# A macaron attention block on one core: the second query group's probabilities are turned by VectorE and transfers instead of TensorE

## The reference

```python
x = x + 0.5 * ffn(layernorm(x))        # 384 hidden, silu(gate) * up
x = x + attention(layernorm(x))        # 16 heads of 64, rotary, causal softmax
x = x + 0.5 * ffn(layernorm(x))
# attention, for each batch and head:
scores = where(causal, q @ k.T * 64 ** -0.5, -inf)
out = softmax(scores) @ v              # then the 16 heads side by side, @ wo.T
```

## Time and profile before

| | |
|---|---|
| median of 3 runs | 1251.76 us (1251.71 to 1252.58) |
| the profiled execution | 1256.88 us |
| its span | 1255.0 us |
| TensorE busy | 1220.6 us (97%), 7,264 matmuls |
| VectorE busy | 734.1 us (58%) |
| ScalarE busy | 892.1 us (71%) |
| GpSimd busy | 401.6 us (32%) |
| transfers | 164.84 MB, mean 131 GB/s |

### The profile page before, as it was taken

The page is one execution under the profiler, slowest core; times in us unless marked ns, Lnnn a source line. Parts: engine busy times, 40 slices in busy tenths (PEclk is TensorE's granted clock), DMA queues, the critical chain, the costliest instruction groups (busy, mean ns, idle before and its releaser), DMA issues. The chain is left out here.

```text
span 1255.0 us, 26509 instructions
## 1 busy us (share of the span) xinstructions
PE 1220.6 (97%) x7264; PEld 845.1 (67%) x7264; DVE 734.1 (58%) x1790; ACT 892.1 (71%) x1945; POOL 401.6 (32%) x223
## 2 busy tenths in 40 slices
PE   7996999999999999999999999999999999999898
PEld 4554776767676767676767777676767676766465
DVE  5565656565656565656566666556555656564454
ACT  4764777777777777777777777677777777777574
POOL 3343423332323333333333332323332333330000
PEclk8997999999999999999999999999999999999999
DMA  6236556565554555555555555546555455543000
GB/s 253 85 120 161 135 127 164 129 170 128 153 143 128 138 144 142 133 142 141 138 139 140 153 128 141 156 119 170 128 157 140 131 138 146 135 101 78 11 35 33
DMA packets 118606, 164.84 MB, mean 131 GB/s; under 512 B 14384, under 2 KB 64432, under 8 KB 118448
## 3 DMA queue, kind: packets, MB, share of 16 engines
q1 hardware_dynamic: 118176, 163.70, 49.2%
q10 hardware_dynamic: 400, 0.79, 0.3%
HBM read 53.02 MB, written 10.75 MB: 51 GB/s over the span
## 5 line engine op out<-in xcount | busy, mean ns | idle before, releaser
L1017 DVE CUSTOM_DVE_ANT_0 probs<-wide,tri_mask 128x1024 f32<-128x1024 f32 (+7 forms) x512 | 382.4, 754 | 251.0 <-PE wide L733 247.5
L922 ACT ACTIVATE shared_a<-bank 128x512 f32<-128x512 f32 (+2 forms) x640 | 338.5, 550 | 165.5 <-PE bank L749 159.6
L911 ACT ACTIVATE probs<-probs,neg_max 128x1024 f32<-128x1024 f32 (+7 forms) x512 | 394.5, 772 | 84.3 <-DVE neg_max L1017 82.1
L749 PEld LDWEIGHTS bank<-ident,probs 128*128 128x128 f32 x2304 | 259.5, 140 | 132.2 <-issue 70.1
L153 POOL TENSOR_TENSOR rotated<-terms,cross 128x1024 f32<-128x1024 f32 x62 | 148.5, 2396 | 613.0 <-DVE cross L147 612.8
L749 PE MATMUL bank<-ident,probs 128*128 128x128 f32 x2304 | 343.5, 278 | 1.1 <-ACT shared_a L922 0.4
L766 PE MATMUL bank<-shared_a,v_cur 128*64 128x256 f32 (+3 forms) x1792 | 297.3, 453 | 0.0
L732 PE MATMUL wide<-k_hh,q_hl 128*128 128x512 f32 (+3 forms) x768 | 288.8, 378 | 7.7 <-DMA k_low<-parts 5.5
L733 PE MATMUL wide<-k_low,q_hl 128*128 128x512 f32 (+3 forms) x768 | 255.7, 345 | 0.0
L766 PEld LDWEIGHTS bank<-shared_a,v_cur 128*64 128x64 f32 x1792 | 108.8, 136 | 121.8 <-issue 85.2
L732 PEld LDWEIGHTS wide<-k_hh,q_hl 128*128 128x128 f32 x768 | 146.3, 191 | 36.3 <-issue 24.1
(11 more groups left out here) (143 smaller groups left out, 1235.6 us busy)
## 6 DMA issues: line engine op xcount, KB each, us to landing
q_hl<-parts SPq DMA_DIRECT2D x254, 128.0 KB, 2.7
k_hh<-parts SPq DMA_DIRECT2D x254, 128.0 KB, 2.7
v_cur<-shared_b SPq DMA_DIRECT2D x32, 512.0 KB, 4.3
inv_sum<-inv_scratch SPq DMA_DIRECT2D x128, 128.0 KB, 3.1
k_low<-parts SPq DMA_DIRECT2D x63, 256.0 KB, 4.2
xn_cur<-xn_scratch SPq DMA_DIRECT2D x15, 1024.0 KB, 6.6
w_qk<-w_scratch SPq DMA_DIRECT2D x32, 256.0 KB, 3.1
w_scratch<-first_w_parts SPq DMA_DIRECT2D x8, 512.0 KB, 3.1
```

The costliest lines, as they stand in the source:

```text
L749: last = nc.tensor.transpose(ring[at % 2][:, col:col + P], probs[g][:, h, OFFSET[g][r] + j * P:OFFSET[g][r] + (j + 1) * P], ident[:])
L911: nc.scalar.activation(own, own, ACT.Exp, bias=neg_max[g][:, col], scale=-1.0, accum_out=sums[g][:, col]).then_inc(probs_done, 1)
L922: nc.scalar.activation(turned[:, slot, to], ring[at % 2][:, 0:w * len(heads)], ACT.Copy).then_inc(ring_free[at % 2], signals)
L1017: nc.vector.tensor_tensor_reduce(out=part_of_probs(g, k), in0=wide_banks[k % 2][:, x0:x1], in1=tri_mask[:, SEQ - (x1 - x0):], scale=1.0, s ...
```

## The change

Group 0 stays as it is, with its ten turns and a ring of 14 places a pair instead of 24. Group 1 has no turns by TensorE and no copies by ScalarE any more:

- `score` writes each unit of group 1 as two halves of equal width, one in each bank of the wide tile. Its keys come in another order: key 128 j + 64 b + 2 i + c goes to bank b, part c, block j, column i. The matmul's moving operand so reads every second float.
- The mask has that order too; VectorE and GpSimd set it up once. Probabilities go to `second`, four parts (b, c) of 32 columns for each block.
- `turn_blocks` on VectorE turns each square of 32 x 32 in place, one instruction for a unit, eight a pair.
- `send_second` on SyncE moves the squares: eight transfers for each of two sets (blocks 4 and 5 of both heads, then blocks 2 and 3), each from 32 partitions to 64, of 2,816 or 1,792 bytes for a partition, into `spread`, 16 transfers a pair.
- `times_v_second` multiplies in three steps, reading `spread` in runs of 32 columns and writing `out_bank` in the order quarter, block, row of the quarter. `normalise` puts the columns back.
- The q and k fills are issued for the whole sequence, 8 transfers a pair instead of 16. The inverses are spread as they lie in DRAM, without reordering.
- The hand-written orders of all four engines are changed to suit.

The core of the diff:

```diff
+def fill_qk_whole(queue, o, u, h):
+    for part in range(2):
+        to = slice(HEAD_DIM * part, HEAD_DIM * (part + 1))
+        queue.dma_start(o.q_hl[u][h][to, :].bitcast(F32), rows_of(o, h, part, slice(0, SEQ))).then_inc(o.filled_qk[u][0], 16)
+        queue.dma_start(o.k_hh[u][h][to, :].bitcast(F32), rows_of(o, 2 + h, 0, slice(0, SEQ))).then_inc(o.filled_qk[u][1], 16)
...
+        SECOND_STEPS = [(0, (0, 1, 2)), (0, (3, 4, 5)), (1, (0, 1, 2, 3))]
...
-                q = q_hl[u][h][:, P * TILES[g][r]:P * (TILES[g][r] + 1)]
-                x0, x1 = scores_at(g, k)
-                for a, b in ((x0, min(x1, CHUNK)), (CHUNK, x1)):
...
+                    else:
+                        high, low = (a[u][h][:, 0:P * n].rearrange("d (j b i c) -> d b c j i", b=2, i=HALF, c=2)[:, b] for a in (k_hh, k_low))
+                        out = wide_banks[k % 2][:, CHUNK * b:CHUNK * b + HEAD_DIM * n].rearrange("p (c j i) -> p c j i", c=2, i=HALF)
+                    nc.tensor.matmul(out, q, high, start=True, stop=False)
+                    last = nc.tensor.matmul(out, q, low, start=False, stop=True)
...
+            def times_v_second(p, u, d):
+                s, blocks = SECOND_STEPS[d]
+                if d == 0:
+                    may_multiply(p, 1)
+                pe.wait_ge(spread_full[s], 16 * SENDS * (p + 1))
+                for j in blocks:
+                    rows = [r for r in SET_ROWS[s] if TILES[1][r] >= j]
+                    for h in range(2):
+                        out = out_bank[HEAD_DIM * h:HEAD_DIM * (h + 1), :].rearrange("p (a r i) -> p a r i", a=QUARTERS, r=4)
+                        out = out[:, :, rows[0], :] if len(rows) == 1 else out[:, :, rows[0]:rows[-1] + 1, :]
+                        last = nc.tensor.matmul(out, v_cur[:, u, j, HEAD_DIM * h:HEAD_DIM * (h + 1)], spread_of(s, h, j, rows),
+                                                start=(j == 0), stop=(j == TILES[1][SET_ROWS[s][1]]))
+                last.then_inc(out_step, 1)
...
+            def turn_blocks(p, k):
+                dve.wait_ge(probs_done, unit(p, 1, k))
+                own = part_of_second(k)
+                nc.vector.transpose(own, own).then_inc(blocks_turned, 1)
...
+            def send_second(p, s):
+                sp.wait_ge(blocks_turned, 8 * p + 4 * (s + 1))
+                if some(p):
+                    settle(sp)
+                    sp.wait_ge(out_step, NK * (p - 1) + (NK - 1, NK)[s])
+                for a in range(QUARTERS):
+                    for b in range(2):
+                        sp.dma_start(spread[s][HEAD_DIM * b:HEAD_DIM * (b + 1), a, :],
+                                     second[s][HALF * a:HALF * (a + 1), 2 * b:2 * b + 2, :]).then_inc(spread_full[s], 16)
```

More of the change, by code:

```diff
@@ L905, in exponential @@
             def exponential(p, g, k):
[L906 removed]
+                h, r = UNITS[g][k]
                 col = slice(4 * h + r, 4 * h + r + 1)
@@ L1084, in pair @@
                 max_of(p, 1, 6)
+                turn_blocks(p, 3)
                 max_of(p, 1, 7)
@@ L1087, in pair @@
                 invert(p, 1)
+                turn_blocks(p, 4)
+                turn_blocks(p, 5)
+                ahead(4)
+                turn_blocks(p, 6)
                 next_max(0)
-                ahead(4)
                 next_max(1)
@@ L1093, in pair @@
                 next_max(3)
+                turn_blocks(p, 7)
                 normalise(p, 0)
@@ L1204, in pair, with next_qk @@
             def pair(i, u, first, last):
                 p = 2 * i + u
-                has_next = not (last and u == 1)
-                if has_next and not (first and u == 0):
-                    may_fill(p + 1)
-                    for c in range(2):
+                has_next, later = not (last and u == 1), not (first and u == 0)
+                def next_qk():
+                    if has_next and later:
+                        may_fill(p + 1)
                         for h in range(2):
-                            fill_qk(sp, o, 1 - u, c, h)
@@ L1212, in pair @@
-                send_inv(p, 0)
-                if has_next and not (first and u == 0):
-                    for h in range(2):
-                        fill_low(sp, o, 1 - u, h)
-                spread_inv(p, 0)
-                if has_next:
-                    copy_v(p + 1, i + u, 1 - u)
-                    if not (first and u == 0):
-                        sp.wait_ge(ring_full, ring_count(p, RING_OUT[1]))
-                    load_wo(1 - u, (2 * i + u + 1) % PAIRS)
-                    if not (last or (last is None and u == 1)):
+                            fill_qk_whole(sp, o, 1 - u, h)
@@ new lines, in next_low, with next_v, next_wo @@
+                def next_low():
+                    if has_next and later:
+                        for h in range(2):
+                            fill_low(sp, o, 1 - u, h)
+                def next_v():
+                    if has_next:
+                        copy_v(p + 1, i + u, 1 - u)
+                def next_wo():
+                    if has_next:
+                        if later:
+                            sp.wait_ge(ring_full, ring_count(p, RING_OUT[1]))
+                        load_wo(1 - u, (2 * i + u + 1) % PAIRS)
@@ L1223, in pair, with next_inputs @@
+                def next_inputs():
+                    if has_next and not (last or (last is None and u == 1)):
                         sp.wait_ge(proj_full, proj_unit(i + 1, u, 5))
```

281 lines of the change are left out of this document (151 added, 130 removed).

## The result

The changed kernel takes 1354.24 us (median of 4 runs, 1348.91 to 1357.99) beside 1252.17 us for the one before. The ratio is 1.081, with a 95% interval of 1.0772 to 1.0848. The forecast was 1147 us, with a range of 1105 to 1215: the sign was wrong.

A forecast was written before the change was run, and what follows sets the result against it. TensorE's instruction stream, 97% busy, was taken as the bound. Terms -118.7 - 15 - 10 + 5 + 3 + 26 + 5 = -104.7 us took the profiled 1256.9 to 1152.2, and a median 5.1 lower gave 1147 us, range 1105 to 1215.

The forecast's parts named there:

- The strided keys: Second group's score matmuls on TensorE: reading every second float taken as free; upper end +4.1 us a pair, 132 us.
- rival 3: TensorE's strided key read runs at half rate: +132 us, 1279 us; at a quarter more per column, 1180; chance 0.07.
- Transfers: Sends and SyncE's queue: 7.0 MB a pair nearly a second bound; late product costs 26 us, between 0 and 70.
- rival 2: Transfers set the pace: at 200 GB/s, 35 us a pair, 1322 us; chance 0.12, half of it mild at 1200 to 1245.
- What goes: TensorE loses 1,152 turning matmuls at 0.103 us, 118.7 us; besides, 15 us at following scores and 10 of ring waits.
- The two smaller terms: On TensorE: 15 us from score matmuls slowed behind turns, 10 us (0 to 49) from fewer waits for ring banks.
- VectorE: Eight in-place turns a pair take 6.2 us (3.9 to 12.4), 0.69 per 512 columns; hidden at 87% busy, with thin cover.
- Rival 1: VectorE becomes the bound: turns of 10 to 12.4 us make the pair 31.3 us, 1204 us in all; chance 0.10.
- Splitting the scores and the products: On TensorE: halved second-group scores cost 5 us, 20 smaller products by V instead of 12 cost 3 (0 to 15).
- the one for rival 3: Sign in the profile after: second-group score matmuls of 384 columns 0.36 us apart instead of 0.18.
- The sign of being wrong: TensorE idle before spread or before scores over 2 us a pair, or VectorE's turns over 1 us per 512 columns.
- the sum without lateness: The forecast's 1147 us less its 26 us for the late product behind the transfers: 1121 us.

The follow-up runs named there:

- keys_in_order: The changed kernel, but the second group's score matmuls read each block's keys as they lie, in runs of 32 floats without the step of two; 1321.4 us.
- alternated: The changed kernel with ScalarE issuing the inverses' transfers and successive transfers ordered to use different partition halves; 1311.9 us.

## Why the prediction was wrong

**The strided keys** ("I take free") is the step that failed first. The reason given was that only the address step changes and the number of columns does not. The row that was missing then is in the profile after: 0.35 us for 384 columns, half rate, and alone it costs 116 us of the 132 that I had put as the upper end. This is rival 3, at a chance of 0.07. The Trainium skill's rule (Advanced Engine Details and Errata, SBUF Cachelines), two hits on a line are enough, does not hold for this read: by it the step is free, and the trace says that it doubles the time. The measurement decides. With 116 us in its place the forecast's sum gives 1147 + 116 = 1263 us, a small loss. One block shows why so little is left: 2 x 128 columns of scores at half rate are 2 x 128 x 0.46 ns = 0.12 us more at the upper end (0.10 as measured), against 0.103 us for the turn that is saved. The other 91 us to 1354 must come from other steps.

**Transfers** ("I count half of the middle, 0.8 us a pair, 26 us in all, between 0 and 70") was mis-sized. Cutting the sends to one eighth is worth 86 us in the changed kernel. The same sends cost 89 us on the kernel before, where no reader waits for them. I had taken 253 GB/s, read from the best 2 us, as the rate; over 900 us the engines moved 194 to 199 in most kernels with whole sends, and 209 at best. The outcome looks like rival 2, but that the rate is the limit is not shown. With 7.0 MB a pair in each of these kernels the mean rate and the pace are one number told twice (keys_in_order: (1230.8 - 132.2) / 31.5 = 34.9 us, 7.0 MB / 34.9 us = 201 GB/s), so a rate near 200 at a pace near 35, or below 213 in a slower kernel, proves nothing. The engines' share was 0.81 and 0.82 with the list on SyncE, and rose to 0.91 when the list got shorter.

What the runs show in its place is two things. One is the path that the forecast left out, **SyncE's list**: it counted issues and landing, but no wait for the inverses' round trip through DRAM, which took 73 us of 900 in the kernel before and takes 126 to 150 in the changed one and keys_in_order. The list thereby has little reserve or none, the first set of sends leaves 5.2 us after its data are ready in the pair shown, and issuing the inverses from ScalarE instead gives 35 us (18 with short sends). The other is the bytes: some 60 of the 89 us on the kernel before. Part of that goes through the list as well: in 900 us SyncE waits 77 us for the round trip with whole sends and 44 with short ones, and TensorE 48 and 26 for k_low, whose own way to landing did not grow (4.2 and 4.0 us). How these two divide the 86 us inside the changed kernel was not separated. Also, the waits of over 1 us for spread in 200 to 1100 us all fall in the even pairs, where the V projections give the product the larger cover (11.7 us by the forecast): a count of TensorE's cover from the last scores to the product didn't say when the list would let the sends go. The Trainium skill's 218 GB/s for one half of the ports (SBUF — State Buffer, Door 1) lies near the rate, but changing the order between the halves gave 7.5 us in one pair of kernels and nothing clear in the other, without a higher rate, so the runs don't bear it out as the cause.

**What goes** (-118.7, and 15 and 10 beside it) was probably mis-sized too. A block left out of the turns gave 0.058 us, not 0.103. Over all 36 blocks that would be 67 us where I had 119, if the rest behaves as these 26 did. But that kernel keeps ScalarE's copies, which the change takes away with the turns, and TensorE waits for them there (11 us in 200 to 1100 us, none before); so 67 us is a hint and no price for the change itself. The two smaller terms were not measured.

**VectorE** was right in size: the turns take (61.9 + 53.5 + 43.1 + 35.5) / 32 = 6.06 us a pair, against 6.2, and 0.67 us for 512 columns. Rival 1 did not happen; turning costs 8 us in the order made for it, with short sends. The same turns cost 74 us in the order of the kernel before, at a busy share of 68%: the share doesn't tell whether they are hidden.

**Splitting the scores and the products** can't be judged from after, where the step and the waits cover it; in keys_in_order the widths keep their pace once running (384 columns 0.18 us apart, 192 columns 0.09 to 0.12, as the forecast had them).

Of the signs named ahead, the one for rival 3 came (0.35 us for 384 columns), and the transfers stayed below 230 GB/s. The sign of being wrong, over 2 us a pair of waiting before spread or before scores, did not come: it is 1.4 and 0.9 us. So this sign was set too high: the kernel was far off with less waiting than that.

The parts do not add. Alone the step, the sends and the turns cost 116, 89 and 74 us. In the changed kernel taking away the step gives 33, since waiting for transfers takes its place, and 38 once the sends are short; in both kernels without the step SyncE's list is full, which fits with a faster TensorE finding the same limit. What is left at the end, 1203.9 against the 1121 of the sum without lateness, fits with 52 us of the smaller gain and the 28 of the issues, but this last reckoning is argued and not shown. No version with the reference's result came below the kernel before; the best of the changed family is alternated, 1311.9 us. A version that reads keys in order and still brings each to its row of V was not run, nor the changed kernel with short sends and the inverses off SyncE's list.

## What to carry to other kernels

Price a new access pattern at both ends before you trust the gain, and compare the upper end with the gain for one block: here 0.12 us against 0.10 would have shown that the whole gain hung on it. Take the rate of transfers from long stretches, not from the best two microseconds, but don't read a mean rate as a limit where it follows from the pace. Count every round trip that a queue waits for in its list; transfers that nobody waits for still delay those that stand behind them. A work item removed from an engine at 97% busy need not give its full pace back (here 0.058 of 0.103 us): try leaving it out first, which costs one run.

## What the runs showed of the hardware that was not expected

- TensorE reads a moving float32 operand of this type with a step of two floats at about 0.9 ns a column, against 0.46 in order, at the same granted clock (1.00). Runs of 32 floats with jumps between them cost nothing that shows.
- The issue of a q fill by SyncE took 0.60 us in the median at 128 KB, with and without 16 more sends a pair on the kernel before, and 0.86 at 256 KB in the changed kernel (0.90 with short sends). So the longer issues appear with the larger fills and not with the sends' bytes; single fills took up to 2.1 us.
- SyncE's wait for a small write to DRAM (inverses of 8 x 128 floats), issued behind the fills, was 1.7 us in the mean and 5.2 at most in the kernel before, 2.6 and 4.7 in the changed one.
- Of TensorE's 12 waits of over 2 us for spread in 200 to 1100 us, 9 were followed by slower matmuls, at the lower granted clock where that was read (0.50 at 739.0 to 739.5 us): the same 12 took 1.7 to 2.8 us instead of 1.5. A late transfer so cost more than its wait. After the other 3, of 2.2 to 2.5 us, they took 1.5.
